# Second expert stage: gate and up weights copied and held stationary, activations made transposed

## The reference, cut to what matters

```
shared = silu(xf @ Sg) * (xf @ Su) @ Sd
probs = softmax(xf @ Wr); topk_p, topk_i = top_k(probs, 2)      # 16 experts
cw[token, topk_i] += topk_p
for each expert (wg [256,128], wu [256,128], wd [128,256], c = cw of this expert):
    y = silu(xf @ wg) * (xf @ wu) @ wd
    acc = acc + y * c[:, None]
return acc + shared
```

## Time and profile before

| | |
|---|---|
| median of 3 runs | 1661.55 us (1661.26 to 1665.26) |
| the profiled execution | 1671.27 us, its span 1669.5 us |
| PE busy | 1512.5 us, 91% of the span, 9897 matmul passes |
| DVE / ACT / POOL busy | 1018.1 (61%) / 736.3 (44%) / 573.8 us (34%) |
| mean granted TensorE clock | 0.943 |
| second expert stage | from its first matmul at 1467.7 us to the next phase's at 1609.8 us |
| its largest groups | PE L1173 82.7 us, POOL L1145 75.9, PE L1188 48.7, DVE L1229 32.7, PE L1166 31.0, ACT L1252 30.3 us |

### The profile page before, as it was taken

One profiled execution on the slowest core, in us unless ns is written; L12 is line 12 of the kernel. 1 busy time (PEld: TensorE's weight loads), 2 busy tenths in 40 slices (PEclk: granted clock), 3 DMA queues, 4 the chain that ended last, 5 costly groups with the idle time before them and its releaser, 6 DMA issues. The chain is left out here.

```text
span 1669.5 us, 31211 instructions
## 1 busy us (share of the span) xinstructions
PE 1512.5 (91%) x9897; PEld 1139.7 (68%) x9897; DVE 1018.1 (61%) x3467; ACT 736.3 (44%) x1537; POOL 573.8 (34%) x993
## 2 busy tenths in 40 slices
PE   5999999984799999799799999999999587489988
PEld 3777777773799999655466666666666376368877
DVE  3344555443244444479798888888887276545558
ACT  3444444420222222245267777777777232244421
POOL 4123333335122222235522332233223165635530
PEclk9999999986899999889899999999999798689999
DMA  7001111113777677669856666666661485745546
GB/s 230 1 26 36 48 45 52 39 39 112 207 214 211 209 211 215 193 225 292 210 77 92 93 91 90 97 96 91 93 92 42 130 256 185 164 128 159 159 154 209
DMA packets 150592, 221.74 MB, mean 133 GB/s; under 512 B 23648, under 2 KB 98144, under 8 KB 150304
## 3 DMA queue, kind: packets, MB, share of 16 engines
q1 hardware_dynamic: 127904, 170.58, 44.0%
q0 software_dynamic: 13344, 36.55, 6.3%
q10 hardware_dynamic: 9184, 12.61, 2.5%
HBM read 141.16 MB, written 78.25 MB: 131 GB/s over the span
## 5 line engine op out<-in xcount | busy, mean ns | idle before, releaser
L1987 ACT ACTIVATE t_probs<-t_ps_st 128x512 f32<-128x512 f32 x576 | 313.2, 596 | 124.8 <-PE t_ps_st L2039 122.3
L1965 DVE CUSTOM_DVE_ANT_0 whole_sum<-t_ps_s,t_later 128x512 bf16<-128x512 f32 (+3 forms) x512 | 285.6, 587 | 13.9 <-PE t_ps_s L2025 11.8
L1941 POOL TENSOR_SCALAR_AFFINE_SELECT t_probs<-t_probs 128x128 f32<-128x128 f32 x512 | 138.3, 304 | 330.1 <-ACT t_probs L1987 328.8
L2025 PE MATMUL t_ps_s<-t_ks,t_qs 96*128 96x512 f32 (+3 forms) x768 | 247.7, 362 | 0.5 <-ACT t_neg_max L1977 0.5
L2039 PE MATMUL t_ps_st<-t_qs,t_ks 128*128 128x512 f32 (+3 forms) x768 | 242.7, 365 | 0.8 <-ACT t_probs L1987 0.8
L2039 PEld LDWEIGHTS t_ps_st<-t_qs,t_ks 128*128 128x128 f32 x768 | 136.8, 189 | 73.7 <-ACT t_probs L1987 40.2
L1965 DVE CUSTOM_DVE_ANT_0 whole_sum<-t_ps_s,t_later,t_first_max 128x512 bf16<-128x512 f32 (+3 forms) x256 | 140.6, 549 | 47.9 <-PE t_ps_s L2025 47.9
L2054 PE MATMUL t_ps_o<-t_probs,t_vs 128*17 128x256 f32 (+1 forms) x2560 | 154.9, 361 | 0.5 <-ACT whole_sum L1994 0.5
L2025 PEld LDWEIGHTS t_ps_s<-t_ks,t_qs 96*128 96x128 f32 x768 | 138.7, 190 | 17.9 <-DVE t_first_max L1965 1.6
L1382 PE MATMUL m_ps_h<-m_xt,m_w_t 128*128 128x128 f32 x1136 | 140.4, 277 | 0.0
L1352 POOL DMA_INDIRECT outputs_dram<-m_y,m_place x71 | 68.2, 961 | 208.4 <-DVE m_place L1427 200.7
(11 more groups left out here) (326 smaller groups left out, 2703.8 us busy)
## 6 DMA issues: line engine op xcount, KB each, us to landing
m_w_t<-in_w_dram SPq DMA_DIRECT2D x71, 512.0 KB, 4.4
t_qs<-qkt_dram SPq DMA_DIRECT2D x128, 128.0 KB, 5.7
t_ks<-qkt_dram SPq DMA_DIRECT2D x128, 128.0 KB, 5.9
m_x_t<-gathered_dram SPq DMA_DIRECT2D x79, 128.5 KB, 2.1
m_x_t<-gathered_dram SPq DMA_DIRECT2D x71, 129.0 KB, 2.2
d_ye<-outputs_dram SPq DMA_DIRECT2D x8, 1024.0 KB, 8.3
qkt_dram<-d_hi ACTq DMA_DIRECT2D x32, 256.0 KB, 5.4
qkt_dram<-d_lo SPq DMA_DIRECT2D x32, 256.0 KB, 7.1
```

The source lines that it names most:

```text
L1941: nc.gpsimd.affine_select(out=diag, in_=diag, compare_op=ALU.is_ge, fill=0.0, base=0, pattern=[[1, P]], channel_multiplier=-1).then_inc(ma ...
L1965: nc.vector.tensor_tensor_reduce(out=seen[:, (NP * p + x) % (RS + 1), 0:keys], in0=bank_of(p, x)[:, 0:keys], in1=masks, scale=1.0, scalar= ...
L1987: nc.scalar.activation(probs[:, p % 2, i // NST, base:base + STC], ps_st[(NX * p + i) % RT][:], ACT.Exp, scale=HD ** -0.5).then_inc(exp_re ...
L2025: nc.tensor.matmul(bank_of(p, x)[:, 0:keys], q[0:MAX_ROW, head, qc * P:(qc + 1) * P], k[0:MAX_ROW, head, k0:k0 + keys], start=True, stop=T ...
```

## The change

`run_experts` goes, and `run_gated_experts` takes its place in the second expert stage. Before the tile's turn ACT copies its expert's gate and up weights (128 x 512 of fp32, at an address that comes from a register) from `wgu_sb` to a ring of three fixed buffers `w_t` (`take_weights`, two tiles ahead; for this ACT looks into the list itself). PE holds blocks of 128x128 of `w_t` stationary and streams `xt`, so that `ps_h` comes out as channels x tokens: block 0 is the gate, block 1 is up. The product that DVE makes is then already `ht`; `turn_h` and `copy_h` are gone, and `go_down(i-2)` stands one turn earlier. `ps_x` has two buffers.

```
-            def turn_x(t):
-                wait(pe, xt_ready, t)
+                wait(pe, xt_ready, t - 1)
...
-            def go_up(t):
-                pe.wait_ge(xt_ready, t + 1)
-                wait(pe, h_ready, t - 1)
-                for j in range(KD):
-                    last = nc.tensor.matmul(ps_h[t % 2][:], xt[:, t % 2, j, :], w_up[:, j, bass.ts(expert[t], width)],
-                                            start=(j == 0), stop=(j == KD - 1))
-            def turn_h(t):
...
+            def go_up(t):
+                pe.wait_ge(w_ready, t + 1)
+                pe.wait_ge(xt_ready, t + 1)
+                wait(pe, h_ready, t - 1)
+                for f in range(2):
+                    for j in range(KD):
+                        last = nc.tensor.matmul(ps_h[t % 2][:, f, :], w_t[:, t % 3, j, f * F1:(f + 1) * F1], xt[:, t % 2, j, :],
+                                                start=(j == 0), stop=(j == KD - 1))
+                last.then_inc(h_done, 1)
+            def go_down(t):
+                pe.wait_ge(h_ready, t + 1)
+                wait(pe, y_ready, t - 1)
+                nc.tensor.matmul(ps_y[t % 2][:, 0:DM], ht[:, t % 2, :], w_down[:, 0, bass.ts(expert[t], DM)],
+                                 start=True, stop=True).then_inc(y_done, 1)
+            for i in range(n_list + 2):
+                if live(i):
+                    turn_x(i)
+                if live(i - 1):
+                    go_up(i - 1)
+                if i % 4 == 3 and live(i + 1):
+                    look_up(i + 1)
+                if live(i - 2):
+                    go_down(i - 2)
...
+            def gate(t):
+                dve.wait_ge(sig_ready, t + 1)
+                nc.vector.tensor_tensor(act_g[:, t % 2, :], ps_h[t % 2][:, 0, :], sig[:, t % 2, :], ALU.mult).then_inc(gated, 1)
+                dve.wait_ge(gated, t + 1)
+                wait(dve, y_done, t - 1)
+                nc.vector.tensor_tensor(ht[:, t % 2, :], ps_h[t % 2][:, 1, :], act_g[:, t % 2, :], ALU.mult).then_inc(h_ready, 1)
+            for i in range(n_list + 2):
+                late(dve, i)
+                if live(i - 1):
+                    take_place(i - 1)
+                    gate(i - 1)
+                if live(i - 2):
+                    finish(i - 2)
...
-            def copy_h(t):
...
+            def take_weights(t):
+                if t % 4 == 0:
+                    expert.update(enumerate(entries(act, t, 0, E - 1), t))
+                wait(act, h_done, t - 2)
+                nc.scalar.activation(w_t[:, t % 3], w_up[:, :, bass.ts(expert[t], 2 * F1)], ACT.Copy).then_inc(w_ready, 1)
+            act.wait_ge(*weights)
+            take_weights(0)
+            take_weights(1)
+            for i in range(n_list + 1):
+                if live(i):
+                    copy_x(i)
+                if live(i - 1):
+                    sigmoid(i - 1)
+                if live(i + 2):
+                    take_weights(i + 2)
```

More of the change, by code:

```diff
@@ L2749, in build @@
               lambda eng: load_moe1_up(eng, moe1_loaded, wgu_sb, w_gu))
-        phase(run_experts, c, "m1_", E1, gathered[1], outputs[1], kept, (2 * F1, wgu_sb, None), (F1 // P, wd_sb, None),
-              (moe1_loaded, 16 * (KD + 1)), lambda dve, i: weights_of_choice(dve, nc, kept, i), by_row=True)
+        phase(run_gated_experts, c, E1, gathered[1], outputs[1], kept, wgu_sb, wd_sb,
+              (moe1_loaded, 16 * (KD + 1)), lambda dve, i: weights_of_choice(dve, nc, kept, i))
         phase(finish, c, outputs[1], kept, total, xnt_all, shared, flat(out))
```

246 lines of the change are left out of this document (86 added, 160 removed).

## The result

| | before | after |
|---|---|---|
| median of 5 runs | 1665.26 us (1661.26 to 1667.06) | 1654.43 us (1650.55 to 1656.03) |
| the profiled execution | 1671.27 us, span 1669.5 | 1650.55 us, span 1648.8 |
| the stage, from its first matmul to the next phase's | 142.1 us (1467.7 to 1609.8) | 130.5 us (1459.1 to 1589.6) |

After over before is 0.9943 (95% interval 0.9923 to 0.9962): 0.57% faster, 0.38 to 0.77%. The two profiled executions differ by 20.7 us, but 8.6 of that lies ahead of the stage, in code that is the same in both. The stage itself is 11.6 us shorter; 7.9 was forecast for it, less a few tenths. Of all executions in this document one stands apart, at 3026.92 us, of before_lookup_early; it is in that kernel's median and in no ratio.

A forecast was written before the change was run, and what follows sets the result against it. PE's throughput was taken to bound the stage. Shorter turns (6.6 us) plus the end (1.3), less a few tenths at the start, gave 7.7 us: 1661.55 - 7.7 = 1653.9 us, eight-in-ten range 1650.5 to 1660.5.

The forecast's parts named there:

- What bounds the stage: In the second expert stage PE, busy 125.49 of 125.90 us, bounds a tile by the columns it streams.
- PE's turn: PE's work per tile: 0.22 + 0.895 + 0.43 = 1.545 us instead of 1.63, saving 6.6 us over 78 turns.
- Look-ups of PE stay as many: PE's list look-ups in each fourth turn: number unchanged, so no gain counted from them.
- ACT: ACT's weight copy occupies 0.52 to 0.6 us, hidden by PE; after a look-up of 0.34 to 0.75, sigmoid up to 0.27 late.
- The chain: From `go_up` to `go_down`'s weight load through sigmoid and DVE's products: 1.27 us, with slack of 0.17 us.
- The start: At the stage's start ACT's first look-up and two copies, 1.8 us, hide beside the rows' 2.16 us: cost nothing.
- The end: From the last `go_up` out to POOL's last send: 3.58 us instead of 4.84, saving 1.26 us.
- Rival 3: In `go_up` the four added weight loads aren't hidden: a turn 0.38 us longer, about 1690 us; chance 0.02.
- The sum in the stage: The stage's total gain: 6.6 + 1.3 = 7.9 us, less a few tenths for slow-clock turns at the start: 7.7.
- Rival 1: The `go_up` to `go_down` chain or ACT's look-ups replace PE as the bound: gain 1.3 to 4.0 us; chance 0.18.

The follow-up runs named there:

- before_lookup_early: The kernel before with only PE's look-up of the list moved from behind `turn_h` to behind `go_up`; median 1662.49 us, ratio 0.9953, stage 139.1 us.

## Why the prediction was right, and where not

- *What bounds the stage*: right. PE 117.10 of 117.10 us busy, and the turn is PE's own work.
- *PE's turn*: right. 0.21 + 0.90 + 0.44 = 1.55, forecast 1.545; `go_up` 0.90 against 0.895.
- *"Look-ups of PE stay as many"*: the step that failed. Their number stayed, their cost didn't. Before, a look-up stood between `turn_h`, which waits for DVE, and `go_down`, with 0.11 us of streaming to hide it; now it stands behind the 0.9 us of `go_up`. The term should have been 0.19 to 0.20 x 19, 3.6 to 3.8 us, on top of 6.6. Together up to 10.4; from the first matmul to the last `go_up` out the stage went from 134.4 to 124.2 us, 10.2 less. before_lookup_early shows the term alone in the other kernel: its stage is 3.6 shorter. The rows for it were in the trace: the prediction put the 0.04 us between 1.63 and the mean of 1.673 down to look-ups (0.04 x 78 = 3 us) and then counted them as still exposed in the new order.
- *ACT*: right. The copy is 0.63 us, and 0.52 from its start to the next instruction's (1521.98 to 1522.50), the lower end of 0.52 to 0.6. A look-up takes ACT 0.31 us (0.34 to 0.75 forecast). The one of 0.85 us did to the sigmoid what the prediction had worked out for 0.75, 0.24 us late (up to 0.27 forecast), and cost 0.06 us.
- *The chain*: right in size. 0.20, then 0.31 and 0.32 for the products (forecast 0.41 and 0.32), and 0.42 to the weight load at the end (forecast 0.34): 1.25 of 1.27. On the first occasion the slack of 0.17 to 0.19 held in all turns of the steady row but that one.
- *The start*: right. First matmul 2.20 us after the rows' transfer began (1456.88 to 1459.08), 2.16 before.
- *The end*: right. 3.48 us, forecast 3.58; saved 1.36 against 1.26.
- *Rival 3*, the added weight loads: refuted for this shape. Eight passes with eight full-array loads take 0.90 us.
The rule in the Trainium skill ("TensorE: Matmul & The Clock Gate", "Part 3: Packing small matmuls") that a load overlaps only a matmul of other row groups doesn't hold for these passes. The same section, which the prediction quoted only in part, also lets a load into the background weight buffer run ahead of matmuls in flight. That would agree with the 0.90 us; no run here tests it.

The sum in the stage is -11.6, where 7.7 was forecast. The median, 1654.43, is 0.5 us from the forecast of 1653.9, and that closeness is partly luck: the kernel before was 3.7 us slower in five runs than in the three shown (1665.26 and 1661.55), which stands against a gain some 3 us larger.

*Rival 1* deserves more than its 0.18. On the first occasion it cost 0.06 us in one turn. On the two on which the changed kernel ran again the chain it names (sigmoid, products, `go_down`) did set one turn in four or five, by a mechanism that no distance in the trace of before showed: signals of PE 1.2 us late against a slack of 0.17. Why they are late is open. There the result of the same change is a loss of 0.5 to 0.7%. And on the second occasion the version to prefer was neither of the two but before_lookup_early: 0.9953 where the changed kernel had 1.0073. The changed kernel on the first occasion, 0.9943, is the fastest measured against its own reference, but the two intervals overlap, and before_lookup_early was not run there.

## What to carry to other kernels

When work is moved on an engine that is the bound, ask of every small instruction that stays (a register load, an address) what stands ahead of it: here it was free behind the 0.9 us of queued passes, and behind an instruction that had just waited it cost 0.2 of its 0.33 us. A tighter turn can bring out delays that no trace of the longer one shows: the same kernel, with 0.17 us to spare in one chain, had a stage of 130.5 us on one occasion and 19 to 26 us more on two others. So a gain of half a per cent should be measured on more than one occasion and chip, and the cheap part of it (here the look-up's place) taken alone.

## What was unexpected of the hardware

- PE's signals to other engines can come about 1.2 us late and in a bunch, while its passes keep their distances (1546.475 for work out at 1545.11). 15 to 21 turns of 78 were long for it in the changed kernel on two occasions and none on the first. With a turn of 1.97 us no signal was late, and the kernel before had 1 or 2 long turns. The cause is open.
- A look-up on PE costs 0.20 us behind `turn_h` and 0.00 behind `go_up`: the same instruction, moved by one place.
- Three kinds of ACT instructions in a row overlap alike, by 0.10 to 0.12 us: copies of 0.63 start 0.52 apart, one of 0.38 makes way after 0.26, a sigmoid of 0.28 after 0.16.
